# The last feed-forward batch of a decoder layer: its sum of squares and operand halves moved, its last rows stored by tile

## The reference

```
h  = silu(gate) * up            # gate, up = x @ ternary(w_gate_up).T, 2048 columns each
hn = h * rsqrt(mean(h*h) + eps) # the mean runs over the 2048 hidden columns of each row
x  = x + hn @ ternary(w_proj).T # back to 512 columns
```

## Time and profile before

| | |
|---|---|
| median of 3 runs | 1321.91 us (1319.98 to 1324.07) |
| the profiled execution | 1320.05 us |
| its span, first to last instruction | 1318.1 us |
| outside the span | 1.95 us |
| mean granted TensorE clock | 0.979 of full |
| TensorE busy | 1223.5 us, 93% of the span |
| VectorE, ScalarE, GpSimd busy | 954.0, 592.5 and 567.5 us |

### The profile page before, as it was taken

The page is one execution under the profiler, slowest core; times in us unless marked ns, Lnnn a source line. Parts: engine busy times, 40 slices in busy tenths (PEclk is TensorE's granted clock), DMA queues, the critical chain, the costliest instruction groups (busy, mean ns, idle before and its releaser), DMA issues.

```text
span 1318.1 us, 20051 instructions
## 1 busy us (share of the span) xinstructions
PE 1223.5 (93%) x7263; PEld 829.8 (63%) x7278; DVE 954.0 (72%) x1294; ACT 592.5 (45%) x702; POOL 567.5 (43%) x484
## 2 busy tenths in 40 slices
PE   3787999999999999999999879999599999999996
PEld 3454555656647556565575457777487877787772
DVE  6889878878878788788787878988536554644443
ACT  2575385674774756747657610000134322432231
POOL 1353243543533535436345439999233222322230
PEclk9899999999999999999999989999799999999998
DMA  8354233533443335424345347783000000000000
GB/s 297 111 153 132 76 96 116 156 93 98 147 143 111 103 103 155 131 86 140 107 143 171 129 96 140 140 158 84 1 1 1 18 17 17 0 16 17 17 1 32
DMA packets 127989, 123.76 MB, mean 94 GB/s; under 512 B 31612, under 2 KB 89218, under 8 KB 127938
## 3 DMA queue, kind: packets, MB, share of 16 engines
q1 hardware_dynamic: 102984, 116.86, 29.3%
q10 hardware_dynamic: 24960, 6.29, 3.4%
HBM read 81.63 MB, written 35.21 MB: 89 GB/s over the span
## 4 chain that ended last, share of the span: by engine, by line
PE 71%; DVE 14%; issue 7%; ACT 4%; DMA 2%; POOL 2%; SPq 0%; DVEq 0%; POOLq 0%; ACTq 0%
PE bank L797 11%; PE bank L842 9%; PE bank L843 9%; PE bank L568 8%; PE bank L569 8%; PE bank L570 8%; PE bank L862 4%; PE bank L861 4%; PE bank L653 2%; PE bank L632 2%; PE bank L631 2%; ACT region_c L954 2%; DVE ctx L1207 2%; ACT rsum L925 1%; DVE rsumT L1199 1%
## 5 line engine op out<-in xcount | busy, mean ns | idle before, releaser
L842 PE MATMUL bank<-h_hi,guT 128*128 128x256 f16 x1024 | 226.2, 274 | 1.4 <-DVE h_lo L1576 1.4
L843 PE MATMUL bank<-h_lo,guT 128*128 128x256 f16 x1024 | 226.1, 274 | 0.0
L1675 POOL TENSOR_TENSOR parts<-parts 128x512 f32<-128x512 f32 x80 | 130.7, 1637 | 190.8 <-DVE parts L1186 190.8
L568 PE MATMUL bank<-hT_hi,w_hi 128*128 128x256 f16 x640 | 177.5, 277 | 17.2 <-DVE w_lo L1251 9.5
L569 PE MATMUL bank<-hT_lo,w_hi 128*128 128x256 f16 x640 | 177.5, 277 | 0.0
L570 PE MATMUL bank<-hT_hi,w_lo 128*128 128x256 f16 x640 | 177.3, 277 | 0.0
L797 PE MATMUL bank<-kv,toep 128*128 128x288 f32 x640 | 158.7, 411 | 4.1 <-ACT qT L993 2.5
L1680 POOL TENSOR_SCALAR_AFFINE_SELECT region_c<-region_c 128x512 f32<-128x512 f32 x128 | 104.2, 838 | 122.5 <-ACT region_c L957 122.5
L797 PEld LDWEIGHTS bank<-kv,toep 128*128 128x128 f32 x640 | 123.1, 193 | 39.3 <-ACT qT L993 3.0
L653 PE MATMUL bank<-region_c,v 128*128 128x512 f32 x256 | 133.8, 604 | 12.2 <-DVE ctx L1207 12.1
L954 ACT ACTIVATE region_c<-bank,cap_scale 128x1536 f32<-128x1536 f32 x64 | 98.6, 1541 | 57.7 <-PE bank L632 57.5
(11 more groups left out here) (144 smaller groups left out, 2517.2 us busy)
## 6 DMA issues: line engine op xcount, KB each, us to landing
unit_halves<-halves SPq DMA_DIRECT2D x80, 256.0 KB, 2.3
q_both<-unit_halves SPq DMA_DIRECT2D x64, 256.0 KB, 3.0
wffn<-w_gu SPq DMA_DIRECT2D x8, 1024.0 KB, 5.5
q_high<-unit_halves SPq DMA_DIRECT2D x64, 128.0 KB, 3.1
toep<-kernel_padded SPq DMA_DIRECT2D x32, 256.0 KB, 4.1
cpair<-ctx_pairs SPq DMA_DIRECT2D x32, 176.0 KB, 4.5
xin<-x SPq DMA_DIRECT2D x8, 512.0 KB, 4.2
region_o<-wq SPq DMA_DIRECT2D x4, 1024.0 KB, 12.0
```

The lines of the kernel that those rows point to most:

```text
L568: pe.matmul(dst, lh, rh, start=first and k == 0, stop=False)
L842: pe.matmul(dst, guT[:, k, col:col + P], h3_hi[:, p, k, :], start=(k == 0), stop=False)
L843: mm = pe.matmul(dst, guT[:, k, col:col + P], h3_lo[:, p, k, :], start=False, stop=(k == DB - 1))
L1675: pool.tensor_tensor(slot[:, 0], slot[:, 0], slot[:, 1], ALU.add).then_inc(unit_summed, 1)
```

## The change

Four things are changed, all behind the last up product.

1. `sum_squares(7)` is put inside `down(6)`, before c = 5, and writes bank 0 in place of bank 4. It no longer waits for `finish(6)`; it still waits for the last addition of the squares.
2. VectorE runs `mean_square(7)` from bank 0 without `finish(6)` ahead of it. `finish(6)` comes behind the second quarter (q = 1) of batch 7's halves.
3. The halves of batch 7 go to `tail_hi` and `tail_lo`, which lie in the memory of the first two of four parts of `guT`, no longer read by then. `down(7)` writes banks 6 and 7.
4. `down(7)` goes through c = 0 to 11 as before, and then does c = 12 to 15 for tile 0 and after that for tile 1, so that tile 0 is whole 8 products earlier. Each tile of batch 7 is stored by its own transfer of 256 KB.

```
+                tail_hi, tail_lo = [guT[:, k, :].bitcast(F16).rearrange("p (c s) -> p c s", c=HB) for k in range(2)]
+        TAIL_SUM_AT, TAIL_BOTH = 5, 3 * HB // 4
...
-            with sp.Fori(0, B) as b:
+            with sp.Fori(0, B - 1) as b:
                 sp.wait_ge(y_done, TT * (b + 1))
                 sp.dma_start(out_t[b], x2r[:, bass.ds(TT * b, TT), :]).then_inc(out_stored, 16)
-            sp.wait_ge(out_stored, 16 * B)
+            for i in range(TT):
+                sp.wait_ge(y_done, TT * (B - 1) + i + 1)
+                sp.dma_start(out_t[B - 1, :, i, :], x2r[:, TT * (B - 1) + i, :]).then_inc(out_stored, 16)
+            sp.wait_ge(out_stored, 16 * (B - 1 + TT))
...
-            def sum_squares(b, p, guarded):
+            def sum_squares(b, p, tail=False):
                 pe.wait_ge(sqsum_done, HB // 2 * (b + 1))
-                if guarded:
+                if not tail:
                     pe.wait_ge(y_done, TT * b)
                 for t in range(2):
-                    mm = pe.matmul(bank[:, 4, 0:S], ones[:], sqsum[:, p, t * S:(t + 1) * S], start=(t == 0), stop=(t == 1))
+                    mm = pe.matmul(bank[:, 0 if tail else 4, 0:S], ones[:], sqsum[:, p, t * S:(t + 1) * S], start=(t == 0), stop=(t == 1))
...
-            def down(b, last=False):
+            def down(b, last=False, tail=False):
+                hi, lo, to = (tail_hi, tail_lo, 6) if tail else (hn_hi, hn_lo, 4)
                 for c in range(HB):
-                    if c == TURN3_AT and not last:
+                    if c == TURN3_AT and not (last or tail):
                         turn_h3(b + 2)
+                    if c == TAIL_SUM_AT and last:
+                        sum_squares(b + 1, 1, tail=True)
                     if c % 4 == 0:
                         pe.wait_ge(hn_lo_done, 4 * b + c // 4 + 1)
...
+                for i in range(TT) if tail else ():
+                    for c in range(TAIL_BOTH, HB):
+                        pe.matmul(bank[:, to + i, :], hi[:, c, i * P:(i + 1) * P], pT[:, c, :], start=False, stop=False)
+                        mm = pe.matmul(bank[:, to + i, :], lo[:, c, i * P:(i + 1) * P], pT[:, c, :], start=False,
+                                       stop=(c == HB - 1))
+                    mm.then_inc(down_filled, 1)
...
-            sum_squares(B - 1, 1, True)
-            down(B - 1, last=True)
+            down(B - 1, tail=True)
...
             for q in range(4):
-                high_hidden(B - 1, 1, q)
+                high_hidden(B - 1, 1, q, tail_hi)
...
-                if not first:
+                if not (first or last):
                     finish(b - 1)
...
-            mean_square(B - 1)
+            mean_square(B - 1, at=0)
             spread_rms(B - 1)
             for q in range(4):
                 scaled(B - 1, 1, q)
-                low_hidden(B - 1, 1, q)
-            finish(B - 1)
+                low_hidden(B - 1, 1, q, tail_hi, tail_lo)
+                if q == 1:
+                    finish(B - 2)
+            finish(B - 1, at=6)
```

More of the change, by code:

```diff
@@ L844, in up @@
                 mm.then_inc(up_filled, 1)
-            def sum_squares(b, p, guarded):
+            def sum_squares(b, p, tail=False):
                 pe.wait_ge(sqsum_done, HB // 2 * (b + 1))
-                if guarded:
+                if not tail:
                     pe.wait_ge(y_done, TT * b)
                 for t in range(2):
-                    mm = pe.matmul(bank[:, 4, 0:S], ones[:], sqsum[:, p, t * S:(t + 1) * S], start=(t == 0), stop=(t == 1))
+                    mm = pe.matmul(bank[:, 0 if tail else 4, 0:S], ones[:], sqsum[:, p, t * S:(t + 1) * S], start=(t == 0), stop=(t == 1))
                 mm.then_inc(sum_filled, 1)
-            def down(b, last=False):
+            def down(b, last=False, tail=False):
+                hi, lo, to = (tail_hi, tail_lo, 6) if tail else (hn_hi, hn_lo, 4)
                 for c in range(HB):
-                    if c == TURN3_AT and not last:
+                    if c == TURN3_AT and not (last or tail):
                         turn_h3(b + 2)
+                    if c == TAIL_SUM_AT and last:
+                        sum_squares(b + 1, 1, tail=True)
                     if c % 4 == 0:
                         pe.wait_ge(hn_lo_done, 4 * b + c // 4 + 1)
-                    for i in range(TT):
-                        pe.matmul(bank[:, 4 + i, :], hn_hi[:, c, i * P:(i + 1) * P], pT[:, c, :], start=(c == 0), stop=False)
-                        mm = pe.matmul(bank[:, 4 + i, :], hn_lo[:, c, i * P:(i + 1) * P], pT[:, c, :], start=False,
+                    for i in range(TT) if not tail or c < TAIL_BOTH else ():
+                        pe.matmul(bank[:, to + i, :], hi[:, c, i * P:(i + 1) * P], pT[:, c, :], start=(c == 0), stop=False)
+                        mm = pe.matmul(bank[:, to + i, :], lo[:, c, i * P:(i + 1) * P], pT[:, c, :], start=False,
                                        stop=(c == HB - 1))
@@ L870, in ffn @@
                     if n == 1 and not first:
-                        sum_squares(b - 1, 1 - p, True)
+                        sum_squares(b - 1, 1 - p)
                     if n == (FIRST_OUT_AT if first else OUT_AT) and not last:
@@ L1110, in square_of, with high_hidden @@
                                ACT.Square).then_inc(square_done, 1)
-            def high_hidden(b, p, q):
+            def high_hidden(b, p, q, hi=hn_hi):
                 act.wait_ge(hn_done, 4 * b + q + 1)
-                act.copy(hn_hi[:, 4 * q:4 * q + 4, :], hid[:, p, 4 * q:4 * q + 4, :]).then_inc(hn_hi_done, 1)
+                act.copy(hi[:, 4 * q:4 * q + 4, :], hid[:, p, 4 * q:4 * q + 4, :]).then_inc(hn_hi_done, 1)
             def ffn(b, p, first=False, last=False):
@@ L1583, in gated, with mean_square @@
                                          1.0 / ACT_SCALE, silu[:, n % 2], ALU.mult, ALU.mult).then_inc(hid_done, 1)
-            def mean_square(b):
+            def mean_square(b, at=4):
                 dve.wait_ge(sum_filled, b + 1)
-                dve.transpose(sumT[:], bank[:, 4, 0:S]).then_inc(sum_turned, 1)
+                dve.transpose(sumT[:], bank[:, at, 0:S]).then_inc(sum_turned, 1)
                 wait_apart(dve, sum_turned, b + 1)
@@ L1601, in scaled, with low_hidden, finish @@
                 dve.tensor_tensor(h, h, rmsT[:].unsqueeze(1).to_broadcast([P, 4, S]), ALU.mult).then_inc(hn_done, 1)
-            def low_hidden(b, p, q):
+            def low_hidden(b, p, q, hi=hn_hi, lo=hn_lo):
                 dve.wait_ge(hn_hi_done, 4 * b + q + 1)
                 rows = slice(4 * q, 4 * q + 4)
-                dve.tensor_tensor(hn_lo[:, rows, :], hid[:, p, rows, :], hn_hi[:, rows, :], ALU.subtract).then_inc(hn_lo_done, 1)
-            def finish(b):
+                dve.tensor_tensor(lo[:, rows, :], hid[:, p, rows, :], hi[:, rows, :], ALU.subtract).then_inc(hn_lo_done, 1)
+            def finish(b, at=4):
                 for i in range(TT):
@@ L1611, in finish @@
                     dve.wait_ge(down_filled, TT * b + i + 1)
-                    dve.scalar_tensor_tensor(tok, bank[:, 4 + i, :], 1.0 / ACT_SCALE, tok, ALU.mult, ALU.add).then_inc(y_done, 1)
+                    dve.scalar_tensor_tensor(tok, bank[:, at + i, :], 1.0 / ACT_SCALE, tok, ALU.mult, ALU.add).then_inc(y_done, 1)
             def ffn(b, p, first=False, last=False):
```

## The result

The changed kernel takes 1309.24 us, the median of six runs (1307.58 to 1311.50); the kernel before, run beside it, 1320.22 (1319.31 to 1324.07, six runs). The ratio is 0.9912 with a 95% interval of 0.9896 to 0.9928: faster by 0.7 to 1.0%, by 9.5 to 13.7 us of 1320.22. The forecast was 1310.5 within 1307.5 to 1314.0.

The account below looks back on a forecast made before the run. TensorE bounds the kernel, with idle time and low clock around down(7) to win back. 8.1 + 2.7 + 0.2 + 0.4 = 11.4 us, so 1321.91 becomes 1310.5 us; range 1307.5 to 1314.

Parts of the forecast that it names:

- The gap: TensorE between down(6) and down(7): with the sum inside down(6), down(7) starts at 1289.02, not 1297.14; 8.1 us less.
- The stall of 0.1: TensorE's wait inside down(6) for the last squares, ahead of the sum; taken as 0.1 us, bounds 0 and 1.3.
- The chain behind the sum: From batch 7's transpose to the first product of down(7): 6.75 us as before, now under down(6).
- The margins: How early batch 7's quarters are ready for down(7): 2.5 us for the first, 1.1 for third and fourth.
- The clock: TensorE in down(7): full clock instead of the low level after idle time; 2.7 us less, bounds 0 and 2.7.
- The last addition: Behind the last product: tile 1's addition no longer queues behind tile 0's, 1.10 us instead of 1.27; 0.2 less.
- The store: End of the kernel: last store of half size, outside the loop, saves 0.4 us, bounds 0 and 0.6.
- the split store doesn't pay: Rival on the last store: fixed cost rules, landing stays 2.8 us; sum 11.0, time 1310.9 us; chance 0.2.
- TensorE waits for the halves: Rival in down(7): late halves make products wait once, costing about 2 us or more; 1312.5 to 1315.2 us; chance 0.1.
- the gap only moves: Rival around down(6): the sum or transpose waits there instead, no measurable change, about 1320 us; chance 0.03.
- the one way to end slower: Rival: clock falls while TensorE is dense; all 128 products of two batches slow would give 1337 us; chance 0.03.

Follow-up runs that it names:

- The filled gap: Kernel before with 32 unread 128x512 products put between the sum of squares of batch 7 and down(7); tail 41.29 us, 2.57 less.

## Why the prediction was right

Three of its four terms were right to 0.1 us, and the fourth was too small.

- **The gap** was forecast at 8.1 and is 8.22. The stall of 0.1 did not come: the squares were in time by 0.15 us. The chain behind the sum was put at 6.75 from the transpose to the first product; after, the first quarter is ready at 1287.42, 6.70 behind the transpose at 1280.72. The margins (2.5 and 1.1) came out as 2.6 and 1.4; that they are real, and that `finish(6)` is what sets the smaller one, is shown by the runs with the sum before c = 7.
- **The clock** was forecast at 2.7 and is 2.68. The filled gap gives 2.6 of it back (2.57 by the tail, 2.62 by the starts) without any other gain.
- **The last addition**: 0.2, measured 0.16.
- **The store** was the mis-sized term: 0.4, between bounds of 0 and 0.6, and it measured 0.94, outside of them. The step that failed is the sentence "a store of the half size may gain 0.5 (the 256 KB row) or nothing (the 128 KB row)". Those rows are of transfers with other shapes, amid other traffic. The prediction saw that size was not all of it and still took the two rows as bounds for this tensor. Stores of this very tensor land in 1.8, 2.0, 2.8 and 4.3 us at 128, 256, 512 and 1024 KB: 0.75 to 0.8 us for each 256 KB from 256 KB up, and 0.2 for 128 KB below. Of the 0.94, about 0.8 is this size: landing 2.0 against 2.8, and the run with one store keeps 3.30 from the last addition to the end, against 2.47. The rest lies ahead of the issue, which comes 0.21 behind the last addition before and 0.03 behind it after, and 0.03 too in the run with one store, which also stands outside the loop. The store of batch 6, still inside it after the change, is issued 0.21 behind its addition (1292.08 to 1292.29). So the place outside the loop brings 0.18, where the prediction had "up to 0.1"; which part of the loop's code takes that time is not shown.

The four add up to 12.0 where 11.4 was forecast; the median moved by 11.0, the ratio says 11.6. By the profiles, what lies between these is ahead of the change: `down(6)` starts anywhere from 1272.55 to 1278.58. So it is partly luck that the median's 11.0 lies so near to 11.4: the spread hid the half microsecond that the store had too little. And 1309.24 against 1310.5 says little about the terms, since the 1321.91 that the forecast started from is itself 1.7 over the 1320.22 of six runs.

**The rivals.** That the split store doesn't pay was wrong, and so was the rule that spoke for it, at this place. The Trainium skill ("DMA: Bandwidth & Descriptors", "Measured") is about throughput, which the last transfer doesn't need: nothing comes behind it. Its fit, 2.0 us plus bytes over 436 GB/s ("Anatomy of one DMA"), is for another queue, and the measurement decides: 2.0 and 2.8 us where it has 2.6 and 3.2. That TensorE waits for the halves did not happen but is near: two blocks later it does. That the gap only moves was wrong, and the clock, the one way to end slower, stayed at 1.00.

## What to carry to other kernels

When the last stage of a loop ends with a long dependent chain (reduce, transpose, power, spread, split), look at what its first link really needs: here it needed only sums that were ready ten microseconds early, and a result bank that happened to be in use. Move the link under the work that stands ahead, as early as its input allows, and check each later hand-over for its margin; an engine's order of work (`finish(6)` here) costs margin too. Behind the last product the bytes of the last transfer are on the path, so make it smaller (down to 128 KB it paid here); and where a change is worth less than the spread of the runs, measure it in the profile from a point that both kernels share.

## What the runs showed of the hardware

- After an idle time of 3.33 us (sum before c = 12) TensorE's products were slow for eight distances of 0.43 in place of 0.2157 us, with 1.7 us lost. After 6.78 us (before) and 6.79 us (sum behind `down(6)`) it was 2.68 and 2.32 us. Across waits of 0.43 and 1.40 us the clock stayed at 1.00.
- A store of this tensor outside the loop is issued 0.03 us behind the addition that it waits for, one inside the loop 0.21 us.
- The places of all starts in the tail repeat to 0.01 us from one execution to the next; what varies lies ahead. One part of it is seen. From the first copy of the convolution's result (`outT` to `hbuf`) to `down(6)` it takes 337.3 to 337.4 us in eight of the thirteen profiled executions (1274.24 - 936.9 before) and 338.5 to 338.7 in five (1275.34 - 936.8 after). The granted clock of the window from 950 to 960 us is 0.95 and 0.83 in the two named, and the up products behind the pause between the two stages have distances of 0.213 us until 950.82 and 953.24, and 0.109 from there: TensorE gets its full clock back at one of two times, and the eleven slow products more are the 1.2 us. Most of the spread comes before that (the first copy is at 935.2 to 939.9) and was not looked into.
